# One list of token-expert pairs and accumulating scatters in the expert part of an attention and mixture-of-experts kernel

## The reference, cut to what matters

```
x = x + xattn(layernorm(x), ctx, ctx)     # x, ctx: 64 x 128 x 256, fp32
  score = softmax(einsum('bci,bcj->bij', k, q) / 16, axis=0)     # over the 64 of the batch
  out   = einsum('bci,bij->bcj', v, score)
x = x + ffn(layernorm(x))                 # as 8192 tokens of 256
  logits  = x @ router_w.T                # 8 experts
  probs   = softmax(top 2 of logits)      # two experts for each token
  hmid    = gelu(x @ w1[e].T + b1[e])     # 512
  y       = hmid @ w2[e].T + b2[e]
  out     = sum over the two experts of probs * y
```

## Time and profile before

| | |
|---|---|
| median of 3 executions | 854.59 us (853.89 to 854.79) |
| the profiled execution | 850.98 us, span 849.2 us |
| granted TensorE clock, mean | 0.945 |

### The profile page before, as it was taken

One profiled execution on the slowest core, in us unless ns is written; L12 is line 12 of the kernel. 1 busy time (PEld: TensorE's weight loads), 2 busy tenths in 40 slices (PEclk: granted clock), 3 DMA queues, 4 the chain that ended last, 5 costly groups with the idle time before them and its releaser, 6 DMA issues. The chain is left out here.

```text
span 849.2 us, 22604 instructions
## 1 busy us (share of the span) xinstructions
PE 751.6 (89%) x5931; PEld 642.1 (76%) x5932; DVE 622.8 (73%) x1520; ACT 388.0 (46%) x716; POOL 565.4 (67%) x737
## 2 busy tenths in 40 slices
PE   6999998799999544999999899999789999999995
PEld 5778886678878443997888787889569887878775
DVE  6998999899999777876666566466356665666664
ACT  3555666376776611444443443234234434434432
POOL 5664777688887305667767777646677676776774
PEclk9999999799999656999999999889899999999998
DMA  7887875368887602445544545534444344344340
GB/s 236 252 261 238 240 226 158 122 206 268 270 266 253 208 17 75 143 160 156 167 149 149 167 153 161 156 101 118 128 139 135 119 126 132 102 128 132 106 133 5
DMA packets 82200, 137.20 MB, mean 162 GB/s; under 512 B 10075, under 2 KB 55140, under 8 KB 82032
## 3 DMA queue, kind: packets, MB, share of 16 engines
q0 software_dynamic: 23104, 68.43, 26.9%
q1 hardware_dynamic: 59056, 68.26, 25.8%
HBM read 94.56 MB, written 47.59 MB: 167 GB/s over the span
## 5 line engine op out<-in xcount | busy, mean ns | idle before, releaser
L1062 ACT ACTIVATE work<-psum,b1T 128x256 f32<-128x256 f32 x312 | 130.7, 470 | 289.0 <-PE psum L682 288.9
L705 PE MATMUL psum<-w2T_high,slots 128*128 x1248 | 212.8, 276 | 15.8 <-issue 9.4
L682 PE MATMUL psum<-work,w1T_high 128*128 128x256 f16 x1248 | 211.7, 275 | 2.5 <-ACT work L1070 2.5
L705 PE MATMUL psum<-w2T_low,slots 128*128 x624 | 172.1, 276 | 0.0
L682 PE MATMUL psum<-work,w1T_low 128*128 128x256 f16 x624 | 171.6, 275 | 0.0
L954 DVE CAST slots<-work 128x512 f16<-128x512 f32 x156 | 70.2, 450 | 116.9 <-ACT work L1062 114.9
L705 PEld LDWEIGHTS psum<-w2T_high,slots 128*128 128x128 f16 x1248 | 117.8, 99 | 38.1 <-issue 23.9
L682 PEld LDWEIGHTS psum<-work,w1T_high 128*128 x1248 | 122.8, 99 | 18.1 <-issue 2.9
L563 PE MATMUL psum<-slots,work 128*128 (+1 forms) x512 | 123.4, 391 | 6.7 <-ACT slots L993 5.9
L528 POOL DMA_INDIRECT slots<-rows_first,slots x86 | 93.5, 1087 | 52.1 <-POOL slots L506 25.9
L563 PEld LDWEIGHTS psum<-slots,work 128*128 128x128 f32 x512 | 93.9, 192 | 31.3 <-issue 15.4
(11 more groups left out here) (125 smaller groups left out, 1108.7 us busy)
## 6 DMA issues: line engine op xcount, KB each, us to landing
work<-in_ctx SPq DMA_DIRECT2D x96, 256.0 KB, 3.5
rows_first<-slots SPq DMA_DIRECT2D x32, 514.0 KB, 3.9
slots<-in_x SPq DMA_DIRECT2D x32, 256.0 KB, 3.9
work<-in_L_ffn_w SPq DMA_DIRECT2D x32, 256.0 KB, 3.2
work<-in_x SPq DMA_DIRECT2D x32, 256.0 KB, 3.1
slots<-rows_first,slots POOLq DMA_INDIRECT x86, 3.7
rows_second<-slots POOLq DMA_INDIRECT x78
slots<-rows_second,slots POOLq DMA_INDIRECT x78, 3.6
```

The source lines that it names most:

```text
L682: mm = pe.matmul(h, w1T[pw][:, f, c, bass.ds(e * P, P)], xT[r2][:, (px * HC + c) * GROUP:(px * HC + c + 1) * GROUP], start=(c == 0 and px ...
L705: mm = pe.matmul(y, act16[r2][pa][:, f * GROUP + s * P:f * GROUP + (s + 1) * P], w2T[pw][:, f, bass.ds(e * DIM, DIM)], start=(f == 0 and p ...
L1062: last = act.activation(act32[r2][:, f * GROUP:(f + 1) * GROUP], psum[:, 2 + 2 * r2 + f // 2, (f % 2) * GROUP:(f % 2 + 1) * GROUP], ACT.Ge ...
```

## The change

- One list instead of two: all 16384 pairs of a token and an expert, by expert, 71 groups (64 and 7), one loop. A column of the one-hots is one of 128: 2 picks times 64 batch rows.
- The row that a gather brings is xn and 8 weights, one for each expert (264 words); the weight of an expert that the token doesn't go to isn't used by its group. x2 is written to the output by a DMA of its own in the attention stage.
- The result of a group goes to a buffer of its own (`y_buf`, 3 groups), and is scattered with an addition in the DMA (`compute_op=ALU.add`) to the output. A token can be in two groups, so a scatter waits until the one before has landed (`x_out`).
- No two rows of one scatter may name the same token, so the empty places of a group's list get tokens of their own (a second, smaller list of 32 columns, `fill`).
- The one-hots are made column by column, with `tensor_scalar`. Indices are read in place, without a copy; GpSimd's program has no loop.

```diff
-GROUPS = TOKENS // GROUP + EXPERTS - 1
+GROUPS = PICKS * TOKENS // GROUP + EXPERTS - 1
...
@@ SyncE, attend @@
+                    sp.wait_ge(a_x2, m + 1)
+                    after(sp, a_x2_out[r], before_it)
+                    sp.dma_start(pair_of(out, m * 2), slot2(m * 2, X2, DIM)).then_inc(a_x2_out[r], 16)
...
-                    sp.dma_start(table_b[bass.ds(m * 2, 2), :, :].rearrange("b c w -> c b w"), slot2(m * 2, 0, ROW)).then_inc(a_stored[r], 16)
+                    sp.dma_start(table_b[bass.ds(m * 2, 2), :, :].rearrange("b c w -> c b w"), slot2(m * 2, XN, FFN_ROW)).then_inc(a_stored[r], 16)
...
@@ GpSimd, behind the attention stage @@
-            pool.iota(tile_no.rearrange("p (n b) -> p n b", b=BATCH), [[1, TILES], [0, BATCH]], base=0, channel_multiplier=0,
-                      allow_small_or_imprecise_dtypes=True).then_inc(r_tileno, 1)
...
-                pool.tensor_copy(ring_idx[:, r * 4:r * 4 + 4], index[:, bass.ds(g * 4, 4)]).then_inc(x_idx, 1)
...
+            pool.wait_ge(r_gather, 1)
+            for i in range(GROUPS + L_G2):
+                if i < GROUPS:
                     for s in range(SUB):
...
+                        pool.indirect_dma_start(row_buf[i % LANES * SUB + s], None, table,
+                                                bass.IndirectOffsetOnAxis(ap=index_in[:, n:n + 1], axis=0)).then_inc(x_rows_in[i % LANES], 16)
+                if i >= L_G2:
+                    g = i - L_G2
+                    if g == 0:
+                        pool.wait_ge(r_scatter, 1)
+                    else:
+
+                        pool.wait_ge(x_out, 16 * SUB * g)
+                    pool.wait_ge(x_sum, g + 1)
                     for s in range(SUB):
...
+                        pool.indirect_dma_start(out_rows, bass.IndirectOffsetOnAxis(ap=index_out[:, n:n + 1], axis=0), y_buf[g % Y_RING * SUB + s], None,
+                                                bounds_check=TOKENS - 1, compute_op=ALU.add).then_inc(x_out, 16)
...
@@ TensorE @@
+            for c in range(COLS):
+                if c % 4 == 0:
+                    pe.wait_ge(r_columns, c // 4 + 1)
+                mm = pe.matmul(psum[:, LIST_BANK, 0:TILES], lane_hot[:, c * P:(c + 1) * P], tile_hot[:, c * TILES:(c + 1) * TILES],
+                               start=(c == 0), stop=(c == COLS - 1))
+            mm.then_inc(r_list, 1)
+            pe.wait_ge(r_fills, 1)
+            for c in range(FILLS):
+                mm = pe.matmul(psum[:, FILL_BANK, 0:TILES], lane_hot[:, c * P:(c + 1) * P], tile_hot[:, c * TILES:(c + 1) * TILES],
+                               start=(c == 0), stop=(c == FILLS - 1))
+            mm.then_inc(r_filled, 1)
...
@@ VectorE @@
-                dve.tensor_tensor(tile_one.rearrange("p (n b) -> p n b", b=BATCH),
-                                  tile_of[:, rnd * BATCH:(rnd + 1) * BATCH].unsqueeze(1).to_broadcast([P, TILES, BATCH]),
-                                  tile_no.rearrange("p (n b) -> p n b", b=BATCH), ALU.is_equal).then_inc(r_ones, 1)
...
+                dve.tensor_scalar(lane_hot[:, c * P:(c + 1) * P], iota16, lane_of[:, c:c + 1], None, ALU.is_equal)
+                last = dve.tensor_scalar(tile_hot[:, c * TILES:(c + 1) * TILES], iota_t, tile_of[:, c:c + 1], mark[:, b:b + 1], ALU.is_equal, ALU.mult)
+                if c % 4 == 3:
+                    last.then_inc(r_columns, 1)
...
+                    after(dve, x_out, (g - Y_RING + 1) * (16 * SUB))
+                    for s in range(SUB):
+                        weight = row_buf[r * SUB + s][:, bass.ds(e + DIM, 1)]
+                        last = dve.tensor_scalar(y_buf[r3 * SUB + s], b2_all[:, bass.ds(e * DIM, DIM)], weight, None, ALU.mult)
...
@@ ScalarE, attend @@
+                    act.activation(ranked[:, r2, :, 0, :], psum[:, 6 + r2, 0:16].rearrange("p (j e) -> p j e", j=2), ACT.Copy).then_inc(a_ranked, 1)
```

More of the change, by code:

```diff
@@ L37 @@
 TOKENS = BATCH * ROWS
+PICKS = 2
 HC = DIM // P
@@ L73, in pipeline @@
         body(whole, k, whole // unroll)
[L76 to L100, removed]
 def live(i, k, lag, count):
@@ L318, in xattn_ffn @@
[L318 to L321, removed]
+        counts = take(EXPERTS)
+        total = take(EXPERTS)
+        count_i = take(EXPERTS).bitcast(I32)
+        blocks = take(EXPERTS)
+        ends = take(EXPERTS)
+        ends_half = take(EXPERTS)
+        base = take(PICKS * EXPERTS)
+        where = take(COLS)
+        where_i = take(COLS).bitcast(I32)
@@ new lines, in xattn_ffn @@
+        tile_i = take(COLS).bitcast(I32)
+        lane_i = take(COLS).bitcast(I32)
+        tile_of = take(COLS)
+        lane_of = take(COLS)
+        ones16 = take(P // 2).bitcast(F16)
+        iota16 = take(P // 2).bitcast(F16)
+        iota_g = take(GROUPS)
+        iota_t = take(TILES // 2).bitcast(F16)
+        mark = take(BATCH)
+        own_token = take(SUB)
+        absent = take(FILLS // 2).bitcast(F16)
+        after_it = take(FILLS)
+        unused = take(FILLS)
+        fill_i = take(FILLS).bitcast(I32)
@@ L322, in xattn_ffn @@
+        filled = take(TILES)
+        before_it = take(TILES)
+        same = take(GROUPS)
+        index_in = take(TILES).bitcast(I32)
+        index_out = take(TILES).bitcast(I32)
         b2_all = take(EXPERTS * DIM)
         assert taken[0] <= 28 * 2 * ROW
-        row_buf = [take(ROW) for _ in range(LANES * SUB)]
+        row_buf = [take(FFN_ROW) for _ in range(LANES * SUB)]
+        y_buf = [take(DIM) for _ in range(Y_RING * SUB)]
         act16 = [[take(FC * GROUP // 2).bitcast(F16) for _ in range(2)] for _ in range(2)]
@@ L929, in _ @@
-            chain(dve.tensor_reduce(owner, past.rearrange("p (n e) -> p n e", e=EXPERTS), AX_X, ALU.add))
-            dve.tensor_scalar(owner_i, owner, float(EXPERTS - 1), None, ALU.min).then_inc(r_owner, 1)
-            indices(0)
-            place_tokens(1)
-            dve.wait_ge(r_b2s, 1)
-            def add_bias(g, r, count, now):
-                e = dve.value_load(owner_i[0:1, bass.ds(g, 1)], min_val=0, max_val=EXPERTS - 1)
-                dve.wait_ge(x_rows_in[r], count)
-                for s in range(SUB):
-                    rows = row_buf[r * SUB + s]
-                    last = dve.scalar_tensor_tensor(rows[:, X2:X2 + DIM], b2_all[:, bass.ds(e * DIM, DIM)], rows[:, PR + now:PR + now + 1],
-                                                    rows[:, X2:X2 + DIM], ALU.mult, ALU.add)
-                last.then_inc(x_bias, 1)
@@ L947, in group @@
-            def group(i, k, n, rnd):
-                if live(i, k, L_G1, ALL):
-                    g, r, r2 = i + k - L_G1, (k - L_G1) % LANES, (k - L_G1) % 2
+            chain(dve.tensor_tensor(base[:, 0:EXPERTS], ends, blocks, ALU.subtract))
+            chain(dve.tensor_tensor(base[:, EXPERTS:], base[:, 0:EXPERTS], counts, ALU.add))
+            pl = place.rearrange("p (r b e) -> p r b e", r=PICKS, e=EXPERTS)
+            chain(dve.tensor_tensor(pl, psum[:, 0:PICKS, :].rearrange("p r (b e) -> p r b e", e=EXPERTS),
+                                    base.rearrange("p (r e) -> p r e", r=PICKS).unsqueeze(2).to_broadcast([P, PICKS, BATCH, EXPERTS]), ALU.add))
@@ new lines, in _ @@
+            for c in range(FILLS):
+                b = c // EXPERTS
+                dve.tensor_scalar(lane_hot[:, c * P:(c + 1) * P], iota16, fill_lane[:, c:c + 1], None, ALU.is_equal)
+                last = dve.tensor_scalar(tile_hot[:, c * TILES:(c + 1) * TILES], iota_t, fill_tile[:, c:c + 1], mark[:, b:b + 1], ALU.is_equal, ALU.mult)
+            last.then_inc(r_fills, 1)
+            by_g = "p (g s) -> p g s"
+            chain(dve.tensor_tensor(same[:, 1:], owner[:, 1:], owner[:, 0:GROUPS - 1], ALU.is_equal),
+                  dve.tensor_scalar(same[:, 0:1], owner[:, 0:1], 0.0, None, ALU.mult))
```

443 lines of the change are left out of this document (202 added, 241 removed).

## The result

The changed kernel takes 882.81 us (881.59 to 884.32, median of 4) where the one before takes 854.24 (850.74 to 854.79, median of 4, on the same chip): a ratio of 1.0344, with an interval from 1.0312 to 1.0377 (95%). Forecast were 814 and "faster"; the time lies inside the range, on the side that had 0.27. The profiled execution took 881.59 us, its span 879.8.

A forecast was written before the change was run, and what follows sets the result against it. GpSimd's queue was taken to bound the group loop, TensorE 0.5 us under it. Loop -62.5 and list +21.7 give -40.8 from 849.2, so 808.4 span; 3.6 more for the median gives 814 us, range 772 to 891.

The forecast's parts named there:

- the side that had 0.27: Sign of the whole change: slower than the kernel before was given 0.27, faster 0.70.
- the chain of landings: Group loop: landing, restart 0.81 us, then first scatter 1.3 us set a step of 6.2 us; chance 0.42.
- rival 2: Group loop: accumulating scatters pace it so slowly that the kernel loses, from a 6.78 us step; 891 us, chance 0.28.
- L: Group loop: landing time counted from the second scatter's start, taken as 4.1 us, bounds 3.07 and 5.8.
- rival 1: Group loop: the landing is hidden and TensorE paces at 5.69 us a step; 778 us, chance 0.25.
- the turn: Between the earlier kernel's two rounds, 13.6 us; it gave a plain scatter's landing of 3.07 us and restart of 0.81.
- Columns: List building on VectorE: 256 one-hot instructions at 0.12 us each, 30.7 us, bounds 0.10 and 0.20 each.
- indices: List building, behind the columns: three instructions on the indices, 0.8 us, and nine small chained ones, 2.2 us.
- fill columns: List building on VectorE: 64 more column instructions for the fill list, 7.7 us.
- fill matmuls: TensorE, ahead of the first transposes: 32 matmuls for the fill list at 0.17 us, 5.4 us.
- TensorE's floor: Group loop: where nothing holds TensorE, its step of 48 matmuls and 8 transposes takes 5.69 us.
- GpSimd's copy as the bound of before: Earlier group loop: GpSimd's queue bounds it, with 5.2 us of DMAs and 1.1 of index copy and restart.

The follow-up runs named there:

- e2: Changed kernel with odd groups' accumulating scatters sent to a second tensor, each scatter waiting for the one two groups back: 866.0 us, ratio 1.0141.
- e1: Changed kernel with plain scatters in place of accumulating ones, every wait kept: 803.77 us, ratio 0.9412.
- e4: Changed kernel with 96 more VectorE instructions ahead of the columns, 16 of each of six operand forms: 893.85 us, one execution.
- e8: Kernel before with GpSimd's program written without a loop and indices read in place, no copy: 813.97 us, ratio 0.955.
- e9: Kernel before with GpSimd's program written without a loop, the copy of indices kept: 853.94 us, ratio 1.0005.
- e5: Changed kernel with the large list's one-hots built by 12 large VectorE instructions, read by TensorE with a stride: 877.8 us, ratio 1.0303.

## Why the prediction was wrong on the sign

**The step that failed.** "Queued behind that wait on GpSimd are its own two scatters ... then the first scatter of the next group, 1.3": the cost of an accumulating scatter on GpSimd was taken from the plain one, 1.0 us, 1.3 with the gap before it. It is 1.62, 1.92 with the gap. The price counts in both things that can pace the loop. In the chain of landings all else came nearly as forecast, 4.83 for 4.91, and the first scatter 1.92 for 1.3 makes the step 6.75 for 6.2. In GpSimd's own sum it makes 6.48 for 5.2, and e2 shows that the step stays at 6.52 when the wait for the landing is relaxed. I had written "four DMAs at 1.3 are 5.2 us, below TensorE's 5.69" and bounded only the landing from both sides, never this price, although rival 2 named it in half a sentence and the last lines of the prediction called 1.3 or more a sign that the constant is wrong. Had the scatter taken 1.0, the numbers measured would make L 3.9 - 0.6 = 3.3 and the chain 3.3 + 0.9 + 1.3 = 5.5, under TensorE, which is rival 1 (worked out, not run). In the loop the miss came to 70 steps of 0.55 us, 38.8 us (unrounded).

**The sign took a second miss, of the list.** With the loop as measured and the first scatter where it was forecast, the span would be 368.2 + 472.8 + 7.9 = 848.9, the time of before. With the list as measured and a step of 6.2 it would be 841. Of the 71.4 us that the forecast was off, 40.5 lie in the loop and its end and 30.9 on the way to the first scatter, most of it the columns (below).

**The chain was right in form, and its L partly by luck.** The 3.07 of the turn was called a scatter of "the same 1 KB rows", but the scatters there write whole rows to `rows_second`, 514 words, 2 KB. A plain scatter of 1 KB rows lands in 2.5 (e1). So the base was 0.6 too high and the addition, 1.4 for 1.0, was 0.4 too low, and L = 3.9 comes out near 4.1. The restart, 0.8 to 0.9 at the end of the loop, is that of the turn. The chain is a second pace, about as long as GpSimd's own sum of 6.5: relaxing it gains only 0.23 us a step (e2). The Trainium skill's "DMA: Bandwidth & Descriptors", "Latency and other measured facts", gives 0.2 to 2 us for a memory access. What the addition adds to the landing beyond GpSimd's time, 1.4 - 0.6 = 0.8 us, lies within that; that it is a memory access isn't shown.

**A reading of the earlier trace rows was off.** The stretch from 429.48 to 436.81 holds five DMAs, not four. From second scatter to second scatter (429.78 to 435.81) the step is 6.03, and copy and restart add 0.83 to the four DMAs, not 1.1. No term of the sum hung on it.

**Columns.** Taken 0.12 each, "near the row that runs back to back"; measured 0.39 / 2 = 0.195. The row I took it from the earlier trace rows is a `tensor_scalar` too, but one with its scalars in the instruction; e4 gives that kind 0.103 to 0.106 and the kernel's kinds 0.16 and 0.227. That is 19.1 us in the list and 5.0 in the fill list. The Trainium skill's "VectorE: DVE Perf Modes", on the TRN2 errata, has a formula that came to 24.5 us for the 256; measured are 49.8. That many small instructions speak against the change was right; the size doesn't hold for these, which read a scalar from SBUF.

**The way there.** The columns begin 8.6 us late. The statistics of x2 in the attention stage (64 on VectorE, L789, before L815) start from 164.3 to 285.9, before from 160.4 to 278.3, and the first instruction of the counting starts at 298.62 for 291.17. So 3.9 us come from the stages before, which I had not costed, and 3.7 from the stage, which I had put at zero, up to +6. About 2 of the 3.9 fall in the stage of the sums, where GpSimd's 31 additions (L468, before L480) take 1.82 us each for 1.68. The large index pattern that I gave 1.5 us back for has gone, and nothing came of it: the last steps wait for ScalarE. What makes these stages longer wasn't taken apart.

The misses in sum, against 808.4: columns' begin +8.6, columns +19.1, indices +1.0, fill columns +5.0, fill matmuls -1.3, first transposes to first scatter -1.5 (15.0 for 16.5); the loop +38.8; second scatter +0.6 and end +1.1. That is +71.4, and the span is 879.8.

**What was right.** TensorE's floor (5.69 forecast, 5.67 in e1), GpSimd's copy as the bound of before (e8, e9), the gathers and VectorE's writes hidden, and that the dearer list doesn't outweigh the loop by itself: e1, with all the columns in it, starts scattering 52.7 us later than before, has a loop of 70 x 5.67 = 396.9 us for 496.5, and takes 804. But the margin was thin: with the first scatter at 399.1, the step at which the changed kernel equals the one before is (849.2 - 7.9 - 399.1) / 70 = 6.32, so my own 6.2 would have brought 8 us, not 40. Rival 2's break-even (6.78) was off by the same miss of the list.

## What to carry to other kernels

When a queue paces a loop, first take out of it what is not the queue's work: a copy of indices behind which it restarts cost this kernel 41 us (e8), most of the 50 that the change would have gained with a free addition (e1). When a change gives an operation a new mode (here an addition inside a DMA), price it twice from both sides, its time on the issuing engine and its time to land, and multiply by its count in a step. When two gains lie on one path ahead of one end, look for the second thing that ends there before they are added.

## What was not expected of the hardware

- An indirect DMA of 128 rows of 1 KB with an addition holds GpSimd for 1.62 us, without one for 1.02 (142 of each, the changed kernel against e1). From its start to its landing it takes 3.9 us in the median (e2), the plain one 2.5 (e1).
- A scatter that waited for a landing starts 0.8 to 0.9 us behind it (the end of the loop; 1.3 once), and a gather behind a small copy of GpSimd's own 0.84. Reading the indices in place takes away the second, not the first.
- `tensor_scalar` on 128 and 142 half-precision elements (e4): 0.103 and 0.106 us from start to start with the scalars in the instruction, 0.16 with one (128 elements) and 0.227 with two (142 elements) read from SBUF.
- Matmuls of 142 columns at the granted clock of 0.50 (e5): 0.124 us with close operands, 0.278 with operands read in strides of 64 elements.
